# Halving the first loads of a two-layer decoder kernel, moving its bias rows to another queue, and storing the last result by batch

## The chip, the cores and the metric

The kernel runs on one core of a Trainium2 chip. Times are device microseconds (us) from the start to the end of one execution; the time of a kernel is the median of its timed runs. A separate execution was taken by the hardware profiler, and every row and duration below comes from that one.

## The reference

Two decoder layers on 8 sequences of 256 tokens by 256 features, in float32. Each layer is self-attention, cross-attention to a context of 120 tokens, and a feed-forward block, each followed by a layer norm of the sum. The change touches the first block alone, and the store of the last one:

```python
def _L0_attn_ref(x, kernel, WO):
    q = jnp.einsum('bsm,hmd->bhsd', x, kernel[0])
    k = jnp.einsum('bsm,hmd->bhsd', x, kernel[1])
    v = jnp.einsum('bsm,hmd->bhsd', x, kernel[2])
    ...
    scores = jnp.einsum('bhsd,bhtd->bhst', q, k) * scale
    attn = jax.nn.softmax(scores, axis=-1)
    out = jnp.einsum('bhst,bhtd->bhsd', attn, v)
...
x = _layernorm(x + _L0_attn_ref(x, L0_attn_kernel, L0_attn_WO), axis=-1)
...
x = _layernorm(x + _L1_ffn_ref(x, ...), axis=-1)
```

There are 16 heads of 64, so each of the three slices of `L0_attn_kernel` is a 256 by 1024 matrix of 1 MB.

## The kernel before

The 8 sequences go through in four passes of two (`NB = 2`, `NI = 4`); a pass holds 512 tokens, that is `T = 4` tiles of 128 tokens, `TS = 2` per sequence. Features stand in `KD = 2` slices of 128. Every engine has its own instruction stream, written out by hand in the order in which it runs; the streams meet at semaphores (`wait_ge`, `then_inc`). Nothing is reordered by a planner.

Before the first pass, the SP queue issues the loads in the order in which it is written (lines 460 to 475): the turned input of the two sequences (`turned_x`, features on the partitions), 256 KB each; then value, query and key weights `wv0`, `wq0`, `wk0`, each in two slices of 512 KB, whose runs in memory are one head's 64 floats; then the context, the input `xa`, the output weights and those of the later blocks of layer 0. A DMA counts 16 on its semaphore. Beside it the ScalarE queue issues five loads (lines 1527 to 1531): three small ones of bias columns, then `rows`, twelve bias and gain rows of 256 floats copied to all 128 partitions (1536 KB), then `scalars`. VectorE waits for `rows` and `scalars` together (`got["rows"]`, line 2089) before it makes six small constants, and after that waits for the first scores.

TensorE starts with `project_first` (line 593). It waits for all of `wv0` and for both halves of `turned_x`, and then makes the values: eight groups of 128 tokens by 512 features, over `n = 0..7` with token tile `t = n // 2` and half of the features `h = n % 2`. A group is two products of 128x128 by 128x512 over the two slices of features; each stands in the trace as two instructions, since the numbers are float32 (32 for the eight groups). Groups go alternately to two PSUM banks, and from the third on each waits until ScalarE has copied the group two before it (`v0_kept`, from `keep_first`, line 1244). Then come eight groups of queries and eight of keys over the full 512 tokens, then the scores, and from there one pass after another. `load_turned_x` of the next pass waits for the last key group of this one.

The last pass ends batch by batch on VectorE (line 2107 on): the norm of sequence 0 is applied, then the sums, the statistics and the norm of sequence 1; each `apply_norm` counts up `normed["out"]`. SP waits for both and stores 512 KB at once (`store`, line 454), and waits for that store.

Of the kernel before, what the change touches and what calls it, by code (L numbers as in the profile page):

```python
# [11 lines left out]
P = 128  # L12
# [32 lines left out]
def decoder(nc, I, out):  # L45
    x = I["x"]
    B, S, D = x.shape
# [3 lines left out]
    KD = D // P  # L51
# [18 lines left out]
    with ExitStack() as es:  # L70
# [3 lines left out]
        def signal(name, per=1):  # L74
            return Signal(es.enter_context(nc.semaphore(name)), per)
# [225 lines left out]

        x_in, xt_in = signal("x_in", 16), signal("xt_in", 16 * NB)
        ctx_in_s = signal("ctx_in", 16 * NB)
        got = {n: signal("got_" + n) for n in ("v0", "qk0", "o0", "x0", "ffn0", "ctx", "attn1", "x1", "ffn1",
                                               "cols", "rows")}
# [149 lines left out]

        @blk.sync
        def _(sp):
            load_turned_x(sp, 0)  # L460
            for n, w in ((2, wv0), (0, wq0), (1, wk0)):
                for k in range(KD):
                    sp.dma_start(w[:, k, :].rearrange("p (h d) -> p h d", h=H),
                                 I["L0_attn_kernel"][n, :, k * P:(k + 1) * P, :].rearrange("h p d -> p h d")
                                 ).then_inc(got["v0" if n == 2 else "qk0"].sem, 16)
            load_ctx(sp, 0)
            load_x(sp, 0)
            wo = I["L0_attn_WO"][0].rearrange("(d j e) m -> e d j m", j=J, e=2)
            for e in range(2):
                sp.dma_start(wo0[e * DH0:(e + 1) * DH0, :, :], wo[e]).then_inc(got["o0"].sem, 16)  # L470
            for n in xw_names:
                sp.dma_start(x0w[n][:, :, :], by_tile(I["L0_xattn_" + n], KD)).then_inc(got["x0"].sem, 16)
            for n, k in (("gate", KD), ("up", KD), ("down", C0)):
                sp.dma_start(wn[n][:, :, :], by_tile(I["L0_ffn_w_" + n], k)).then_inc(got["ffn0"].sem, 16)
            load_turned_x(sp, 1)
            sp.wait_ge(w_rounded.sem, 3)
            for n in ("Wk1", "Wk2", "Wv1", "Wv2"):
                sp.dma_start(c_w[n][:, :, :], by_tile(I["L1_xattn_" + n], KD)).then_inc(got["ctx"].sem, 16)
            for n in ("Wv", "Wo"):
                sp.dma_start(m_w[n][:, :, :], by_tile(I["L1_attn_" + n], KD)).then_inc(got["attn1"].sem, 16)  # L480
            sp.dma_start(w1[:, :, :], by_tile(I["L1_attn_W1"], KD)).then_inc(got["attn1"].sem, 16)
            sp.dma_start(w2[:, :, :], by_tile(I["L1_attn_W2"], C1)).then_inc(got["attn1"].sem, 16)
            for e, n in enumerate(("Wf", "Wi")):
                for k in range(KD):
                    sp.dma_start(wfi[:, k, e:e + 1], I["L1_attn_" + n][k * P:(k + 1) * P, :]).then_inc(got["attn1"].sem, 16)
            for n in ("Wq", "Wo"):
                sp.dma_start(c_w[n][:, :, :], by_tile(I["L1_xattn_" + n], KD)).then_inc(got["x1"].sem, 16)
            for t, n, k in ((n_w1, "cn_w1", KD), (n_w2, "cn_w2", KD), (g_w1, "gc_w1", KD)):
                sp.dma_start(t[:, :, :], by_tile(I["L1_ffn_" + n], k)).then_inc(got["ffn1"].sem, 16)
            for t, n in ((n_w3, "cn_w3"), (n_w4, "cn_w4"), (g_w2, "gc_w2"), (g_w3, "gc_w3")):  # L490
                sp.dma_start(t[:, :], I["L1_ffn_" + n]).then_inc(got["ffn1"].sem, 16)

            load_x(sp, 1)
            load_ctx(sp, 1)

            for it in range(1, NI - 1):
                load_turned_x(sp, it + 1)
                store(sp, it - 1)
                load_x(sp, it + 1)
                load_ctx(sp, it + 1)  # L500
            store(sp, NI - 2)
            store(sp, NI - 1)
            sp.wait_ge(out_sent.sem, 16 * NI)


        @blk.tensor
        def _(pe):
# [84 lines left out]

            def project_first():

                pe.wait_ge(got["v0"].sem, 16 * KD)
                for n in range(2 * T):
                    if n == 0:
                        pe.wait_ge(xt_in.sem, 16 * NB)
                    elif n > 1:
                        pe.wait_ge(v0_kept.sem, n - 1)  # L600
                    t, h = n // 2, n % 2
                    for k in range(KD):
                        mm = pe.matmul(bank(7 - n % 2), turned_x[:, k, t * P:(t + 1) * P],
                                       wv0[:, k, h * 512:(h + 1) * 512], start=(k == 0), stop=(k == KD - 1))
                    mm.then_inc(v0_done.sem, 1)
                pe.wait_ge(got["qk0"].sem, 16 * 2 * KD)
                for j in range(J):
                    if j < 2:
                        pe.wait_ge(v0_kept.sem, 2 * T - 1 + j)
                    else:  # L610
                        pe.wait_ge(q0_kept.sem, j - 1)
                    for k in range(KD):
                        mm = pe.matmul(bank(7 - j % 2), wq0[:, k, j * P:(j + 1) * P], turned_x[:, k, :],
                                       start=(k == 0), stop=(k == KD - 1))
                    mm.then_inc(q0_done.sem, 1)
                for j in range(J):
                    if j < 2:
                        pe.wait_ge(q0_kept.sem, J - 1 + j)
                    else:
                        pe.wait_ge(k0_kept.sem, j - 1)  # L620
                    for k in range(KD):
                        mm = pe.matmul(bank(7 - j % 2), wk0[:, k, j * P:(j + 1) * P], turned_x[:, k, :],
                                       start=(k == 0), stop=(k == KD - 1))
                    mm.then_inc(k0_done.sem, 1)
# [586 lines left out]
        def _(act):  # L1211
# [32 lines left out]
            def keep_first():  # L1244
                for n in range(2 * T):
                    act.wait_ge(v0_done.sem, n + 1)
                    act.copy(v0[:, n // 2, n % 2 * 512:(n % 2 + 1) * 512], bank(7 - n % 2)).then_inc(v0_kept.sem, 1)
                for j in range(J):
                    act.wait_ge(q0_done.sem, j + 1)
                    act.mul(q0[:, j, :], bank(7 - j % 2), W0).then_inc(q0_kept.sem, 1)  # L1250
                for j in range(J):
                    act.wait_ge(k0_done.sem, j + 1)
                    act.copy(k0[:, j, :, :].rearrange("p b s -> p (b s)"), bank(7 - j % 2)).then_inc(k0_kept.sem, 1)
# [273 lines left out]
            act.dma_start(cols[:, :], I["cols"]).then_inc(got["cols"].sem, 16)  # L1527
            act.dma_start(n_b3[:, :], I["L1_ffn_cn_b3"].rearrange("(p c) -> p c", c=1)).then_inc(got["cols"].sem, 16)
            act.dma_start(g_b2[:, :], I["L1_ffn_gc_b2"].rearrange("(p c) -> p c", c=1)).then_inc(got["cols"].sem, 16)
            act.dma_start(rows[:, :, :], I["rows"].partition_broadcast(P)).then_inc(got["rows"].sem, 16)  # L1530
            act.dma_start(scalars[:, :], I["scalars"].partition_broadcast(P)).then_inc(got["rows"].sem, 16)
            def one_pass(it, last=None, then=None):
                attn0(it, last)
# [785 lines left out]
```

## Time and profile before

| | us |
|---|---|
| timed runs: median (lowest to highest) of 3 | 1265.72 (1265.17 to 1266.19) |
| the profiled execution: its own time | 1278.1 |
| its span | 1275.9 |
| TensorE busy in it | 1075.6 (84%) |
| VectorE busy | 765.4 (60%) |
| ScalarE busy | 649.0 (51%) |
| GpSimd busy | 331.1 (26%) |
| TensorE's mean granted clock, share of full | 0.922 |

The profiled execution took 2.2 us outside its span and is 12.4 us longer than the median of the timed runs. Differences of before and after are looked for in its span; a duration of it need not be that of a timed run to the last tenth. In the rows below PE is TensorE, PEld its weight loads, DVE VectorE, ACT ScalarE, POOL GpSimd, and SPq and ACTq the queues that issue DMAs. "Idle before" names what ended an engine's wait. PEclk is the granted clock as a share of the full 2.4 GHz. Matmuls overlap, so the start-to-start distance, not the duration, is what one costs.

### The profile page before, as it was taken

What the parts mean: (1) busy time and instruction counts of PE and PEld (TensorE: products, weight loads), DVE (VectorE), ACT (ScalarE), POOL (GpSimd) and SP (SyncE); (2) the same over time, 40 slices, a digit from 0 to 9 for tenths busy, and PEclk for the clock granted to TensorE, in tenths of its full rate; (3) what the DMA queues carried; (4) which work ended last, traced back from release to release, by engine and by line L of the source; (5) the groups of instructions that cost most, each with busy time, mean ns of one, the idle gap of its engine ahead of it and who ended that gap; (6) DMA issues with size and microseconds to landing.
All of it is one profiled execution on the core that took longest, in us unless ns stands there. A gap on an engine that the chain in (4) does not pass through costs nothing.

```text
span 1275.9 us, 19390 instructions
## 1 busy us (share of the span) xinstructions
PE 1075.6 (84%) x7058; PEld 692.6 (54%) x7058; DVE 765.4 (60%) x1834; ACT 649.0 (51%) x1744; POOL 331.1 (26%) x670
## 2 busy tenths in 40 slices
PE   5987988899879998899788998899778987788874
PEld 2454645674545654585454655585454664475452
DVE  0177476556647558565847657664856747864655
ACT  1465345247347744546647734554637724544622
POOL 1056301231115520222025530221124630131012
PEclk9988999897689999999989999998899998998676
DMA  9302200000000000000000000000000000000000
GB/s 238 132 2 90 62 1 9 1 0 2 1 1 18 18 17 1 8 1 1 1 1 18 18 17 2 8 1 1 1 1 1 18 1 2 1 1 1 1 1 17
DMA packets 30446, 22.76 MB, mean 18 GB/s; under 512 B 16656, under 2 KB 29456, under 8 KB 30224
## 3 DMA queue, kind: packets, MB, share of 16 engines
q1 hardware_dynamic: 29760, 19.93, 5.7%
q10 hardware_dynamic: 592, 1.59, 0.3%
q8 instruction: 57, 0.93, 0.3%
q14 instruction: 37, 0.30, 0.1%
HBM read 19.42 MB, written 2.10 MB: 17 GB/s over the span
## 4 chain that ended last, share of the span: by engine, by line
PE 59%; DVE 18%; ACT 11%; issue 5%; POOL 4%; DMA 1%; SPq 0%; POOLq 0%; DVEq 0%; ACTq 0%
PE PS L542 8%; PE PS L529 4%; PE PS L690 4%; PE PS L929 4%; ACT work L1445 4%; PE PS L589 3%; POOL work L2149 3%; PE PS L778 3%; PE PS L572 3%; PE PS L659 2%; PE PS L942 2%; PE PS L676 2%; PE PS L903 2%; PE PS L977 2%; PE PS L641 2%
## 5 line engine op out<-in xcount | busy, mean ns | idle before, releaser
L2123 POOL TENSOR_TENSOR rstd<-var,minus_half 128x2 f32<-128x2 f32 x64 | 45.8, 715 | 464.1 <-DVE var L1569 464.1
L1445 ACT ACTIVATE work<-PS,nmax 120x256 f32<-120x256 f32 x256 | 117.7, 489 | 44.8 <-DVE nmax L1984 44.5
L2149 POOL TENSOR_SCALAR work<-work,inv 128x256 f32<-128x256 f32 x256 | 125.3, 507 | 0.0
L1984 DVE TENSOR_REDUCE nmax<-PS 120x2 f32<-120x512 f32 x128 | 82.0, 685 | 71.0 <-PE PS L929 70.8
L1628 DVE TENSOR_REDUCE nmax<-PS 128x2 f32<-128x512 f32 x128 | 82.2, 684 | 67.3 <-PE PS L641 67.2
L1261 ACT ACTIVATE work<-PS,nmax 128x256 f32<-128x256 f32 x256 | 118.1, 482 | 4.1 <-DVE nmax L1628 4.0
L2118 POOL TENSOR_TENSOR pool_pause<-minus_half 128x1 f32<-128x1 f32 x96 | 30.1, 314 | 263.1 <-DVE inv L1635 138.7
L929 PE MATMUL PS<-x_room 32*120 32x256 f32 x512 | 72.7, 462 | 14.9 <-ACT work L1445 11.2
L676 PE MATMUL PS<-work 128*64 128x256 f32 x512 | 71.2, 400 | 9.6 <-DVE work L1639 9.5
L641 PE MATMUL PS<-work 64*128 64x256 f32 x512 | 72.7, 400 | 1.9 <-ACT work L1261 1.9
L929 PEld LDWEIGHTS PS<-x_room 32*120 32x120 f32 x512 | 44.5, 207 | 41.9 <-issue 33.1
L690 PE MATMUL PS<-wo,work 128*128 128x256 f32 x256 | 60.9, 392 | 2.7 <-ACT work L1271 2.7
L659 PEld LDWEIGHTS PS<-ident,work 64*128 64x128 f32 x1024 | 38.4, 144 | 41.3 <-POOL work L2149 35.2
L1639 DVE COPY work<-PS 128x512 f32<-128x512 f32 x64 | 43.9, 685 | 27.6 <-PE PS L659 27.2
L659 PE MATMUL PS<-ident,work 64*128 64x64 f32 x1024 | 47.4, 235 | 13.8 <-POOL work L2149 12.9
L1267 ACT COPY work<-PS 128x512 f32<-128x512 f32 x64 | 37.6, 588 | 40.7 <-PE PS L659 40.0
L977 PE MATMUL PS<-work,late 128*128 128x256 f32 x96 | 33.9, 486 | 29.0 <-ACT work L1473 29.0
L1735 DVE TENSOR_REDUCE maxx<-PS 128x8 f32<-128x960 f32 x32 | 36.9, 1153 | 34.7 <-PE PS L749 34.6
L942 PE MATMUL PS<-work,v1p 120*32 120x256 f32 x512 | 42.2, 455 | 18.2 <-ACT work L1445 9.6
L1217 ACT COPY turned_a<-PS 128x512 f32<-128x512 f32 x24 | 14.2, 591 | 84.0 <-PE PS L512 84.0
L1445 ACT ACTIVATION_READ_ACCUMULATOR work<-PS,nmax 120x1 f32 x256 | 56.6, 221 | 0.0
L1261 ACT ACTIVATION_READ_ACCUMULATOR work<-PS,nmax 128x1 f32 x256 | 54.7, 214 | 0.0
(278 smaller groups left out, 2441.3 us busy)
## 6 DMA issues: line engine op xcount, KB each, us to landing
turned_x<-in_xT_dram SPq DMA_DIRECT2D x8, 256.0 KB, 3.1
xa<-in_x_dram SPq DMA_DIRECT2D x4, 512.0 KB, 4.5
out_dram<-x_room SPq DMA_DIRECT2D x4, 512.0 KB, 3.0
rows<-in_rows_dram ACTq DMA_DIRECT2D x1, 1536.0 KB, 8.3
late<-in_L_attn_W_dram SPq DMA_DIRECT2D x2, 768.0 KB, 8.0
wv<-in_L_attn_kernel_dram SPq DMA_DIRECT2D x2, 512.0 KB, 11.3
wq<-in_L_attn_kernel_dram SPq DMA_DIRECT2D x2, 512.0 KB, 7.8
wk<-in_L_attn_kernel_dram SPq DMA_DIRECT2D x2, 512.0 KB, 7.5
```

Source lines behind the costliest of these rows:

```text
L542: mm = pe.matmul(bank(n)[:, (t % 2) * width:(t % 2 + 1) * width], lhs[:, k, t * P:(t + 1) * P], weight[:, k, :], start=(k == 0), stop=(k = ...
L641: mm = pe.matmul(bank(2 * (u % 2) + hh)[:, st * S:(st + 1) * S], q0[rows, j, b * S + st * P:b * S + (st + 1) * P], k0[rows, j, b, :], star ...
L659: mm = pe.transpose(bank(4 + g)[:, place:place + 64], e0[rows, u % 2, st, hh, tt * P:(tt + 1) * P], ident[rows, rows])
L676: mm = pe.matmul(bank(6)[hh * DH0:(hh + 1) * DH0, b * S:(b + 1) * S], v0[:, TS * b + tt, (2 * j + hh) * DH0:(2 * j + hh + 1) * DH0], e0t[: ...
L690: mm = pe.matmul(bank(t // 2)[:, (t % 2) * D:(t % 2 + 1) * D], o0t[:, j, t * P:(t + 1) * P], wo0[:, j, :], start=(j == 0), stop=(j == J - 1))
L929: mm = pe.matmul(bank(SCORE_1[r])[0:M, kv * S:(kv + 1) * S], k1m[g % 2][rows, kv, par, :], q1[rows, c, b * S:(b + 1) * S], start=True, sto ...
L942: mm = pe.matmul(bank(2)[32 * r:32 * r + 32, g % 2 * S:(g % 2 + 1) * S], v1p[:, par, r, kv, :, :], e1[:, par, r, kv, :], start=(par == 0 a ...
L1261: op = act.activation(e0[:, u % 2, st, hh, :], bank(2 * (u % 2) + hh)[:, st * S:(st + 1) * S], ACT.Exp, bias=nmax0[:, u % 2, hh, st:st + 1 ...
L1445: op = act.activation(e1[:, par, r, kv, :], bank(SCORE_1[r])[0:M, kv * S:(kv + 1) * S], ACT.Exp, bias=nmax1[:, par, r, kv:kv + 1], accum_o ...
L1628: dve.tensor_reduce(nmax0[:, u % 2, hh, :], bank(2 * (u % 2) + hh).rearrange("p (t s) -> p t s", t=TS), AX.X, ALU.max, negate=True).then_i ...
L1984: dve.tensor_reduce(nmax1[:, par, r, :], bank(SCORE_1[r])[0:M, :].rearrange("p (v s) -> p v s", v=2), AX.X, ALU.max, negate=True).then_inc ...
L2149: op = pool.tensor_scalar(e0[:, u % 2, st, hh, :], e0[:, u % 2, st, hh, :], inv0[:, u % 2, hh, st:st + 1], 1.0, ALU.mult, ALU.mult)
```

## The change

SP now issues the first half of `turned_x` (sequence 0) and the value weights of heads 0 to 7 in two DMAs of 256 KB, all three counting on a new semaphore `opening`; behind them sequence 1 and the value weights of heads 8 to 15; then the query and key weights as before, and then `rows`, which leaves the ScalarE queue. TensorE makes the four token tiles for the first half of the features, then the four for the second; it waits for `opening` at group 0, for sequence 1 at group 2 and for the other half of the weights at group 4. ScalarE copies the groups to where they now belong. The last result is stored sequence by sequence.

```diff
@@ -301,7 +301,7 @@
 
 
 
-        x_in, xt_in = signal("x_in", 16), signal("xt_in", 16 * NB)
+        x_in, xt_in, opening = signal("x_in", 16), Signal(es.enter_context(nc.semaphore("xt_in")), 16 * NB, -16), signal("opening")
         ctx_in_s = signal("ctx_in", 16 * NB)
         got = {n: signal("got_" + n) for n in ("v0", "qk0", "o0", "x0", "ffn0", "ctx", "attn1", "x1", "ffn1",
                                                "cols", "rows")}
@@ -457,12 +457,20 @@
 
         @blk.sync
         def _(sp):
-            load_turned_x(sp, 0)
-            for n, w in ((2, wv0), (0, wq0), (1, wk0)):
+            for half in range(2):
+                sp.dma_start(turned_x[:, :, half * S:(half + 1) * S], I["xT"][half].rearrange("(k p) s -> p k s", p=P)
+                             ).then_inc((xt_in if half else opening).sem, 16)
+                for k in range(KD):
+                    heads = slice(half * H // 2, (half + 1) * H // 2)
+                    sp.dma_start(wv0[:, k, half * 512:(half + 1) * 512].rearrange("p (h d) -> p h d", h=H // 2),
+                                 I["L0_attn_kernel"][2, heads, k * P:(k + 1) * P, :].rearrange("h p d -> p h d")
+                                 ).then_inc((got["v0"] if half else opening).sem, 16)
+            for n, w in ((0, wq0), (1, wk0)):
                 for k in range(KD):
                     sp.dma_start(w[:, k, :].rearrange("p (h d) -> p h d", h=H),
                                  I["L0_attn_kernel"][n, :, k * P:(k + 1) * P, :].rearrange("h p d -> p h d")
-                                 ).then_inc(got["v0" if n == 2 else "qk0"].sem, 16)
+                                 ).then_inc(got["qk0"].sem, 16)
+            sp.dma_start(rows[:, :, :], I["rows"].partition_broadcast(P)).then_inc(got["rows"].sem, 16)
             load_ctx(sp, 0)
             load_x(sp, 0)
             wo = I["L0_attn_WO"][0].rearrange("(d j e) m -> e d j m", j=J, e=2)
@@ -499,8 +507,11 @@
                 load_x(sp, it + 1)
                 load_ctx(sp, it + 1)
             store(sp, NI - 2)
-            store(sp, NI - 1)
-            sp.wait_ge(out_sent.sem, 16 * NI)
+            for b in range(NB):
+                sp.wait_ge(normed["out"].sem, normed["out"].at(NI - 1, b + 1))
+                sp.dma_start(out[(NI - 1) * NB + b].rearrange("(t p) d -> p t d", p=P), y[:, TS * b:TS * b + TS, :]
+                             ).then_inc(out_sent.sem, 16)
+            sp.wait_ge(out_sent.sem, 16 * (NI + 1))
 
 
         @blk.tensor
@@ -592,13 +603,16 @@
 
             def project_first():
 
-                pe.wait_ge(got["v0"].sem, 16 * KD)
                 for n in range(2 * T):
+                    h, t = n // T, n % T
                     if n == 0:
-                        pe.wait_ge(xt_in.sem, 16 * NB)
-                    elif n > 1:
+                        pe.wait_ge(opening.sem, 16 * (1 + KD))
+                    if n == TS:
+                        pe.wait_ge(xt_in.sem, 16)
+                    if n == T:
+                        pe.wait_ge(got["v0"].sem, 16 * KD)
+                    if n > 1:
                         pe.wait_ge(v0_kept.sem, n - 1)
-                    t, h = n // 2, n % 2
                     for k in range(KD):
                         mm = pe.matmul(bank(7 - n % 2), turned_x[:, k, t * P:(t + 1) * P],
                                        wv0[:, k, h * 512:(h + 1) * 512], start=(k == 0), stop=(k == KD - 1))
@@ -1244,7 +1258,7 @@
             def keep_first():
                 for n in range(2 * T):
                     act.wait_ge(v0_done.sem, n + 1)
-                    act.copy(v0[:, n // 2, n % 2 * 512:(n % 2 + 1) * 512], bank(7 - n % 2)).then_inc(v0_kept.sem, 1)
+                    act.copy(v0[:, n % T, n // T * 512:(n // T + 1) * 512], bank(7 - n % 2)).then_inc(v0_kept.sem, 1)
                 for j in range(J):
                     act.wait_ge(q0_done.sem, j + 1)
                     act.mul(q0[:, j, :], bank(7 - j % 2), W0).then_inc(q0_kept.sem, 1)
@@ -1527,7 +1541,6 @@
             act.dma_start(cols[:, :], I["cols"]).then_inc(got["cols"].sem, 16)
             act.dma_start(n_b3[:, :], I["L1_ffn_cn_b3"].rearrange("(p c) -> p c", c=1)).then_inc(got["cols"].sem, 16)
             act.dma_start(g_b2[:, :], I["L1_ffn_gc_b2"].rearrange("(p c) -> p c", c=1)).then_inc(got["cols"].sem, 16)
-            act.dma_start(rows[:, :, :], I["rows"].partition_broadcast(P)).then_inc(got["rows"].sem, 16)
             act.dma_start(scalars[:, :], I["scalars"].partition_broadcast(P)).then_inc(got["rows"].sem, 16)
             def one_pass(it, last=None, then=None):
                 attn0(it, last)
```

How SP's queue stands at the start of the program, before:

```order
L443 DMA turned_x<-in_xT_dram 128x2x256 x2
L463 DMA wv0<-in_L0_attn_kernel_dram 128x16x64 x2
L463 DMA wq0<-in_L0_attn_kernel_dram 128x16x64 x2
L463 DMA wk0<-in_L0_attn_kernel_dram 128x16x64 x2
L451 DMA ctxt<-in_ctxT_dram 128x2x120 x2
L436 DMA xa<-in_x_dram 128x4x256
L470 DMA wo0<-in_L0_attn_WO_dram 64x8x256 x2
```

and now:

```order
L461 DMA turned_x<-in_xT_dram 128x2x256
L465 DMA wv0<-in_L0_attn_kernel_dram 128x8x64 x2
L461 DMA turned_x<-in_xT_dram 128x2x256
L465 DMA wv0<-in_L0_attn_kernel_dram 128x8x64 x2
L470 DMA wq0<-in_L0_attn_kernel_dram 128x16x64 x2
L470 DMA wk0<-in_L0_attn_kernel_dram 128x16x64 x2
L473 DMA rows<-in_rows_dram 128x3072
L451 DMA ctxt<-in_ctxT_dram 128x2x120 x2
```

The two loads of `wv0` became four of half the size with half of `turned_x` between them, and `rows` stands between the key weights and the context.

TensorE's first groups with what they wait for, before:

```order
L603 MATMUL PS<-wv0,turned_x 128x512 [waits xt_in,got_v0]
L603 MATMUL PS<-wv0,turned_x 128x512 x3
L603 MATMUL PS<-wv0,turned_x 128x512 [waits v0_kept]
L603 MATMUL PS<-wv0,turned_x 128x512
L603 MATMUL PS<-wv0,turned_x 128x512 [waits v0_kept]
```

and now:

```order
L617 MATMUL PS<-wv0,turned_x 128x512 [waits opening]
L617 MATMUL PS<-wv0,turned_x 128x512 x3
L617 MATMUL PS<-wv0,turned_x 128x512 [waits v0_kept,xt_in]
L617 MATMUL PS<-wv0,turned_x 128x512
L617 MATMUL PS<-wv0,turned_x 128x512 [waits v0_kept]
L617 MATMUL PS<-wv0,turned_x 128x512
L617 MATMUL PS<-wv0,turned_x 128x512 [waits v0_kept,got_v0]
```

Number, size and place of the products are the same; the first waits for half of the loads, and two later ones wait for the rest.

## Rows read from the trace of the kernel before

**Rows 1.** Chain of work that ended last, 0 to 70 us: start, length, what

```profile
1.78 0.46 SPq L463
...
2.29 11.98 DMA wv<-in_L_attn_kernel_dram
...
14.31 16.46 PE PS L603 x32
30.77 13.73 PE PS L613 x32
44.50 13.73 PE PS L622 x32
58.24 1.11 PE PS L641 x8
```

**Rows 2.** DMA issues of short stretches from 0.7 us: sizes, us from issue to landing

```profile
turned_x<-in_xT_dram SPq DMA_DIRECT2D x1, 256.0 KB, 3.0
...
wv<-in_L_attn_kernel_dram SPq DMA_DIRECT2D x1, 512.0 KB, 10.6
...
wv<-in_L_attn_kernel_dram SPq DMA_DIRECT2D x1, 512.0 KB, 12.0
...
rows<-in_rows_dram ACTq DMA_DIRECT2D x1, 1536.0 KB, 8.3
...
wk<-in_L_attn_kernel_dram SPq DMA_DIRECT2D x1, 512.0 KB, 7.5
...
late<-in_L_ffn_w_down_dram SPq DMA_DIRECT2D x1, 1024.0 KB, 14.2
```

**Rows 3.** Issues in order of time: start, length of issue, queue and line

```profile
0.79 0.94 SPq L443 DMA_DIRECT2D turned_x<-in_xT_dram  x2
1.78 6.18 SPq L463 DMA_DIRECT2D wv<-in_L_attn_kernel_dram  x2
...
2.48 0.60 ACTq L1530 DMA_DIRECT2D rows<-in_rows_dram  x1
...
13.98 4.69 SPq L463 DMA_DIRECT2D wk<-in_L_attn_kernel_dram  x2
...
28.54 1.21 SPq L474 DMA_DIRECT2D late<-in_L_ffn_w_down_dram  x1
```

**Rows 4.** Stretches of 2 us: busy by engine, PEclk, DMA share, GB/s last

```profile
4.00:6.00 2.00, 0.00 (x0) 0.00 (x0) 0.00 (x0) 0.00 (x0) 0.97 (x6) 1.00 0.82 189
6.00:8.00 2.00, 0.00 (x0) 0.00 (x0) 0.00 (x0) 0.00 (x0) 0.00 (x0) 1.00 1.05 396
8.00:10.00 2.00, 0.00 (x0) 0.00 (x0) 0.00 (x0) 0.00 (x0) 0.00 (x0) 1.00 0.98 404
...
42.00:44.00 2.00, 2.00 (x6) 0.85 (x5) 0.00 (x0) 0.60 (x1) 0.00 (x0) 1.00 0.01 3
```

**Rows 5.** TensorE's weight loads and ScalarE's copies at the start, in order of time

```profile
17.89 0.33 PEld L603 LDWEIGHTS PS<-wv,turned_x 128*128 128x128 f32 x1 [0.52 <-issue]
...
18.74 0.33 PEld L603 LDWEIGHTS PS<-wv,turned_x 128*128 128x128 f32 x1 [0.52 <-issue]
19.45 0.19 PEld L603 LDWEIGHTS PS<-wv,turned_x 128*128 128x128 f32 x1 [0.38 <-issue]
19.47 0.59 ACT L1247 COPY work<-PS 128x512 f32<-128x512 f32 x1
20.11 0.39 PEld L603 LDWEIGHTS PS<-wv,turned_x 128*128 128x128 f32 x2 [0.47 <-ACT work L1247]
...
25.66 0.58 ACT L1247 COPY work<-PS 128x512 f32<-128x512 f32 x1 [1.13 <-PE PS L603]
...
27.37 0.58 ACT L1247 COPY work<-PS 128x512 f32<-128x512 f32 x1 [1.13 <-PE PS L603]
```

**Rows 6.** VectorE's first work, and its first read of the feed-forward weights

```profile
59.33 2.48 DVE L1628 TENSOR_REDUCE nmax<-PS 128x2 f32<-128x512 f32 x4 [46.94 <-PE PS L641]
...
70.94 2.28 DVE L1602 TENSOR_REDUCE w_sum<-late 128x1 f32<-128x2048 f32 x1
```

**Rows 7.** The end of the program in order of time: norms and the last store

```profile
1266.89 0.74 DVE L1575 TENSOR_SCALAR x_room<-res,mv,rstd 128x256 f32<-128x256 f32 x2 [0.40 <-POOL rstd L2123]
...
1271.82 0.74 DVE L1575 TENSOR_SCALAR x_room<-res,mv,rstd 128x256 f32<-128x256 f32 x2 [0.81 <-POOL rstd L2123]
1272.59 0.38 SPq L456 DMA_DIRECT2D out_dram<-x_room  x1
```

**Rows 8.** DMA view of 1270 to 1276 us: rates in 40 slices, and the store

```profile
GB/s 0 0 0 0 0 0 0 0 0 0 0 0 0 0 0 0 0 0 0 0 0 0 0 157 348 355 335 355 355 335 362 341 335 212 7 0 0 0 0 0
...
out_dram<-x_room SPq DMA_DIRECT2D x1, 512.0 KB, 2.9
```

## The prediction

> **What bounds the kernel now.** I read the chain of waits first. Its head is [rows 1]: from 2.29 to 14.27 us the program waits for the second load of the value weights, and from 14.31 us TensorE works without a gap through values (16.46 us), queries (13.73) and keys (13.73) until the scores begin at 58.24. So the start of the program is bound by one landing, and then by TensorE. Next the DMA view: which transfers stand ahead of that landing and how fast they go [rows 2 to 4]. Then TensorE and ScalarE at the start, to see when the third and the fifth group are due, since these get new waits [rows 5]. Then who else reads what was loaded [rows 6], and last the end of the program [rows 7, 8]. Everything between the scores of the first pass and the last norm is left as it was, so the question is how much earlier the first matmul can start, whether this arrives at the end, and what the last store gives.
>
> **The change part by part.**
>
> Why the weights land at 14.3 now. SP issues the two inputs from 0.79 us, and the weights at 1.78 and 2.29 [rows 1, 3]. They land at 1.78 + 10.6 = 12.4 and 2.29 + 12.0 = 14.3 [rows 2]. The bytes alone don't explain it: inputs and value weights are 1.5 MB. In 4 to 6 us the DMAs moved 189 GB/s, in 6 to 10 us 396 and 404 [rows 4]; the jump is the 1536 KB of bias rows, issued at 2.48 and landed at 2.48 + 8.3 = 10.8 [rows 2, 3]. The weights come in runs of 256 bytes, the bias rows in runs of 12 KB, and while these pass, the weights hardly move.
>
> Start of TensorE, after. It needs one input half and two quarters of the weights, 256 + 512 KB, and nothing large beside them. The first input was issued at 0.79 and landed 3.0 us later, at 3.8 [rows 2, 3]; it stays first. The 512 KB of weights (524,288 bytes) follow it in the queue, at the 189 GB/s of 4 to 6 us, the stretch with weights in it before the bias rows [rows 4]: 2.8 us, so 6.6 us. The bounds: at the 404 GB/s of 8 to 10 us they take 1.3 us, hence 5.1. On the late side I take the landing that the whole first slice of 512 KB had, 12.4, and subtract only what the bias rows take at about 400 GB/s, 1,572,864 bytes / 400 = 3.9: 8.5 us. Its bytes are as many as the two quarters now. I take 6.6, since the 189 GB/s is for just these runs at just this place; the second key slice, at the end of a long line of such runs, supports it: two of them take 4.69 us to issue, with the queue full [rows 3], 2.35 us for 512 KB. The gain is 14.3 - 6.6 = **7.7 us** (5.8 to 9.2).
>
> The new waits inside the values cost nothing. Before, the third group started at 20.11, 5.8 us after the first, when ScalarE's first copy ended [rows 5]; later groups are 1.71 apart (copies at 25.66 and 27.37 [rows 5]). So group 2 is due at 6.6 + 5.8 = 12.4 and group 4 at 6.6 + 5.8 + 2 x 1.71 = 15.8. Behind the opening there are 256 KB of input and 512 KB of weights, which at the same 189 GB/s take 1.4 and 2.8 us: they are in at 8.0 and 10.8. The cover is 4.4 and 5.0 us; if it were gone, what is late would be lost one for one. What is queued behind these waits is TensorE's whole stream, and ScalarE's copies wait for it.
>
> Order of groups. 32 instructions before, 32 after, with the same operands' shapes; two banks in turn, the same copies on ScalarE of 0.58 us against 1.71 us per group. Nothing.
>
> Query and key weights. The key weights are issued by 18.7 [rows 3], and the last lands some 7.5 us [rows 2] after the middle of that, at about 24; nothing new stands ahead of them, and the bias rows no longer share the engines. Queries are due at 6.6 + 16.5 = 23.1, keys at 36.8, and the query weights went ahead of the key weights by 1 MB, that is by 4.7 us: at 19. The cover shrinks from 11 to 4 us, and stays.
>
> Bias rows. On ScalarE's queue an issue of 0.60 us goes [rows 3], before anything ScalarE has to do. On SP's, it stands ahead of context, input, output weights and the rest. All those loads together end when they did, since the bytes are the same: by 42 us the DMA share is 0.01 [rows 4], the last, w_down, lands at 28.54 + 14.2 = 42.7 [rows 2, 3]. VectorE now waits for the bias rows until about 28 instead of 12; its next work is due at 59.33 - 7.7 = 51.6 [rows 6]. The feed-forward weights are first read at 70.94 - 7.7 = 63.2 [rows 6]. So the cover is 20 us and the cost is nothing.
>
> From there on every event waits, directly or over others, for TensorE's first groups, so all moves by 7.7 us.
>
> Clock. At the start weight loads are 0.85 us apart until 18.74, and from 19.45 on their duration is 0.19 instead of 0.33 [rows 5]: TensorE runs at 1.2 GHz for some 5.1 us after its first matmul and then at 2.4 (the PEclk of that stretch doesn't show it). It idles before it now as it did then, so I keep the values phase at 16.46 us, 2.73 more than the queries. If the slow stretch is absent or twice as long, the start is 2.7 better or worse; a third of that is what I allow. The Trainium skill, TensorE: Matmul & The Clock Gate (part 1, the HAM clock gate), says that the number of slow matmuls at a kernel's start differs from run to run of one kernel. One trace can't show that; the timed runs, 1.0 us apart, leave little room for it, and the sum would be the same.
>
> Last store. It was issued at 1272.59 and landed 2.9 us later; its bytes moved from about 1273.4 to 1275.1 at 335 to 362 GB/s [rows 7, 8]. Now the first sequence is ready at 1266.89 + 0.74 = 1267.6, five us earlier, and only 256 KB are left at 1272.59. At 350 GB/s they take 0.75 instead of 1.5 us; issue and the time after the last byte stay. Gain **0.7 us**; at worst nothing, at best half of the 2.9, 1.4. The Trainium skill, DMA: Bandwidth & Descriptors (anatomy of one DMA), has a fixed part of about 2.0 us and the bytes at 436 GB/s. By it a store of 524,288 bytes takes 3.2 us (the trace: 2.9) and the halving is worth an estimated 0.6. The same formula for the opening's 786,432 bytes from 0.79 us would give 4.6 us and a sum 2.0 us lower than mine; there the rows contradict, since runs of 256 bytes went at 189 GB/s.
>
> **Sum.** 7.7 + 0.7 = 8.4 us off the profiled span of 1275.9: 1267.5. That execution is 12.4 us longer than the median, but neither term is one that its clock could have stretched: both are DMA times. So 1265.72 - 8.4 = **1257.3 us**.
>
> **The rivals.**
>
> Fast opening: with the bias rows gone the small runs go at what the queue reached in 8 to 10 us, the first matmul is at 5.1. Gain 9.2 + 0.7: 1255.8. Against it, the 189 GB/s stretch held next to none of the bias rows. 8%.
>
> Slow opening: the first slice's landing carried a delay of its own, not the bias rows' alone, and the opening is at 8.5 or later. Gain 5.8 + 0.7: 1259.2. For it: between 4 and 6 us the engines were only 0.82 busy, so the transfers were held by something. 10%.
>
> Nothing arrives: the bias rows delay something behind them on SP that the first pass waits for. It would have to be 20 us late for the feed-forward weights. Then the first pass gets back what it gained, and 1265.0 remains. 4%.
>
> Slower: the clock. If the earlier and broken-up start keeps TensorE at 1.2 GHz through the values, each of the 32 instructions costs 0.85 instead of 0.43 us: 27.2 instead of 16.46, 10.7 more, against 8.4 gained: 1268.0. It decides where some 20 of them more than before are slow. Against it: the cover of 4.4 and 5.0 us leaves no new gap, so TensorE does just what it did after its start before. 3%.
>
> **How the numbers follow.** The forecast, an opening between 5.5 and 8 us and a shift that arrives whole, has 75%: 1256 to 1259. The two other openings have 18%, the rest 7%. For the range I go from the fast opening with 1.4 us for the store and 0.9 for the clock, 1265.7 - 9.2 - 1.4 - 0.9 = 1254.2, to the slow one with nothing for the store and 0.9 for the clock, 1265.7 - 5.8 + 0.9 = 1260.8. 0.2% is 2.5 us, about what a measurement of this kernel can tell from no change. All three openings are faster by more than this: 0.93. Within it are the case in which nothing arrives and very late openings: 0.04. Slower: 0.03.
>
> **What the profile after would show.** The first matmul near 6.6 us, waiting for `wv` or `turned_x`; no idle time of TensorE by a DMA at the third and fifth group; the values again 16.5 us, scores at 50.5; VectorE's wait for `rows` ending near 28 and followed by a wait for TensorE; DMA share near zero again from 42; a store of 256 KB at about 1267.6 less the shift, and one that lands near 2.2 us after its issue. I would be wrong if the 256-byte runs at the head of the queue go slower alone than beside others, if sequence 1's input or the other half of the weights ended a wait of TensorE, or if the later passes in the new profile took longer than in the old.

## The result

The changed kernel took 1258.42 us (median of 20 runs), the kernel before 1266.66 (20 runs of its own). The ratio is 0.9942, with a 95% interval from 0.9915 to 0.9968: 7.3 us faster, between 4.1 and 10.8. The prediction was 8.4 us off, to 1257.3, in a range from 1254.2 to 1260.8.

| | before | after |
|---|---|---|
| profiled execution: time | 1278.1 | 1251.83 |
| its span | 1275.9 | 1249.7 |
| TensorE's mean granted clock | 0.922 | 0.940 |
| first matmul | 14.31 | 6.92 |
| values take | 16.46 | 16.43 |
| first scores | 58.24 | 50.82 |
| last store, issue to landing | 2.9 | 2.1 |

The two spans differ by 26.2 us, three times what the timed runs give. The difference that the change made is seen at both ends. First the chain of waits of after, its first 52 us (start, length, what); these lines answer to [rows 1]:

```profile
1.78 5.09 DMA wv<-in_L_attn_kernel_dram
...
6.92 3.79 PE PS L617 x4
...
10.79 1.28 ACT L1261
...
12.08 0.59 ACT work L1261
...
12.81 10.54 PE PS L617 x24
23.35 13.73 PE PS L627 x32
37.08 13.73 PE PS L636 x32
50.82 1.11 PE PS L655 x8
```

The wait for the value weights ends at 6.88 instead of 14.27 us. Queries and keys take 13.73 us each as before, so the scores come 7.42 us earlier. The small pieces between 10.7 and 12.8 are ScalarE's table load and first copy, on which the third group waits; in [rows 5] they stood at the same distance from the start.

The rates of the DMAs of after, in stretches of 2 us (columns as in [rows 4], GB/s last):

```profile
4.00:6.00 2.00, 0.00 (x0) 0.00 (x0) 0.00 (x0) 0.00 (x0) 0.99 (x6) 1.00 1.05 194
6.00:8.00 2.00, 1.08 (x2) 0.56 (x3) 0.00 (x0) 0.00 (x0) 0.00 (x0) 1.00 1.21 282
8.00:10.00 2.00, 2.00 (x4) 0.95 (x3) 0.00 (x0) 0.00 (x0) 0.00 (x0) 1.00 1.36 218
...
18.00:20.00 2.00, 2.00 (x6) 0.95 (x5) 0.00 (x0) 0.63 (x2) 0.00 (x0) 1.00 1.13 351
20.00:22.00 2.00, 2.00 (x6) 0.86 (x5) 0.00 (x0) 0.87 (x2) 0.00 (x0) 1.00 1.02 381
```

194 GB/s while the opening is loaded, then 218 for long stretches of 256-byte runs; the 400 GB/s of 6 to 10 us are gone, and the bias rows pass from 18 to 22 us instead. VectorE waited for them until 23.7 us, and this held nothing up: its first work after that wait, and its first work on scores, 28 us later, as [rows 6] before:

```profile
23.73 0.15 DVE L2104 TENSOR_SCALAR half_b<-scalars 128x1 f32<-128x1 f32 x1 [21.48 <-DMA rows<-in_rows_dram]
...
51.91 2.48 DVE L1641 TENSOR_REDUCE nmax<-PS 128x2 f32<-128x512 f32 x4 [27.70 <-PE PS L655]
```

Last, the end of after: the DMA view of 1244 to 1250 us, in 40 slices as in [rows 8], with the norm ahead of the store:

```profile
1246.38 0.73 DVE L1588 TENSOR_SCALAR x_room<-res,mv,rstd 128x256 f32<-128x256 f32 x2 [0.81 <-POOL rstd L2136]
...
GB/s 0 0 0 0 0 0 0 0 0 0 0 0 0 0 0 0 0 0 0 0 0 0 0 0 0 0 41 287 348 348 369 301 55 0 0 0 0 0 0 0
...
out_dram<-x_room SPq DMA_DIRECT2D x1, 256.0 KB, 2.1
```

The bytes of the last store move for some 0.8 us instead of 1.6, at the same rate, and it lands 2.1 us after its issue.

**Where the other 18 us of the spans went.** Each timed execution comes with its mean granted clock. Over 179 executions of eleven kernels (the two of this study and the nine variants below; for the 20 runs of before beside the result no clock is on record, so its 71 here come from the later sessions) I fitted one span per kernel and one slope for all: a mean clock lower by 0.01 goes with a span longer by 10.0 us (plus or minus 0.3), and what remains is 0.9 us per execution. Slow executions (over 1.5% above the fastest of their kernel; 16 of 195) are left out of the ratios and of this fit; with them the slope is the same and no gain below moves by more than 0.4 us. In one kernel's 20 executions the clock went from 0.922 to 0.941 and the span from 1268.2 to 1249.2. So 0.018 of clock between the two profiled executions is 18 us, and 26.2 - 18 = 8.2 us are the change's; 7.4 + 0.8 at the two ends. In this way, "at equal clock" below, the kernel after is 8.1 us faster (7.7 to 8.5) over 31 executions against 71 of before: 7.9 +- 0.5 from the 19 beside the result, 8.3 +- 0.5 from the 12 of the repetition. The slope is a relation among executions, not an experiment on the clock.

### The profile page after: what moved, and what is told of

Same layout as the page of the kernel before. It is cut to its first block, busy times and chain, and to the rows that moved or that the text cites. A ratio compares the mean times of both kernels' runs of the same rounds, so it can differ in the third digit from the quotient of the medians.

```text
span 1249.7 us, 19394 instructions
## 1 busy us (share of the span) xinstructions
PE 1056.4 (85%) x7058; PEld 683.4 (55%) x7058; DVE 764.8 (61%) x1834; ACT 649.8 (52%) x1744; POOL 331.5 (27%) x670
## 4 chain that ended last, share of the span: by engine, by line
PE 58%; DVE 19%; ACT 12%; issue 6%; POOL 4%; DMA 0%; SPq 0%; POOLq 0%; DVEq 0%; ACTq 0%
PE PS L553 8%; PE PS L540 4%; PE PS L704 4%; ACT work L1459 4%; PE PS L943 4%; POOL work L2162 3%; PE PS L600 3%; PE PS L583 3%; PE PS L792 3%; PE PS L673 2%; PE PS L917 2%; PE PS L690 2%; PE PS L956 2%; PE PS L991 2%; PE PS L655 2%
## 5 line engine op out<-in xcount | busy, mean ns | idle before, releaser
L943 PE MATMUL PS<-x_room 32*120 32x256 f32 x512 | 68.3, 437 | 16.3 <-ACT work L1459 12.5
L1231 ACT COPY turned_a<-PS 128x512 f32<-128x512 f32 x24 | 14.2, 592 | 84.0 <-PE PS L523 83.9
L1588 DVE TENSOR_SCALAR x_room<-res,mv,rstd 128x256 f32<-128x256 f32 x96 | 36.3, 420 | 30.6 <-POOL rstd L2136 30.6
```

The costliest lines, as they stand in the source:

```text
L943: mm = pe.matmul(bank(SCORE_1[r])[0:M, kv * S:(kv + 1) * S], k1m[g % 2][rows, kv, par, :], q1[rows, c, b * S:(b + 1) * S], start=True, sto ...
```

## The experiments

All gains are against the kernel before. "At equal clock" is the fitted value with its 95% interval.

| kernel | first matmul | scores | ratio of timed runs | gain at equal clock |
|---|---|---|---|---|
| before | 14.31 | 58.24 | | |
| bias rows moved alone | 10.30 | 54.13 | 0.9967 (0.9929 to 1.0006) | 4.3 +- 0.6 |
| halves alone | 11.78 | 56.18 | 0.9951 (0.9902 to 1.0000) | 3.1 +- 0.7 |
| store by batch alone | 14.61 | 58.44 | 0.9995 (0.9946 to 1.0045) | 0.9 +- 0.7 |
| after | 6.92 | 50.82 | 0.9942 (0.9915 to 0.9968) | 8.1 +- 0.4 |
| after, again | 7.26 | 51.64 | 0.9941 (0.9920 to 0.9962) | (in the line above) |
| other half of the weights last | 8.08 | 56.31 | 0.9985 (0.9940 to 1.0031) | 4.5 +- 0.6 |
| bias rows late on ScalarE's queue | 6.95 | 51.69 | 0.9934 (0.9902 to 0.9966) | 6.9 +- 0.6 |
| with extra products | 7.87 | 49.97 | 0.9888 (0.9830 to 0.9945) | 9.7 +- 0.7 |
| wait by slice | 5.26 | 49.71 | 0.9945 (0.9910 to 0.9981) | 10.2 +- 0.6 |
| slice and three extra products | 5.06 | 49.60 | 0.9894 (0.9833 to 0.9956) | 10.2 +- 0.8 |
| slice, five products, early table | 5.47 | 47.53 | 0.9929 (0.9892 to 0.9965) | 10.8 +- 0.6 |

**The bias rows alone.**

```diff
-            act.dma_start(rows[:, :, :], I["rows"].partition_broadcast(P)).then_inc(got["rows"].sem, 16)
...
+            sp.dma_start(rows[:, :, :], I["rows"].partition_broadcast(P)).then_inc(got["rows"].sem, 16)
             load_ctx(sp, 0)
```

> The kernel before with one edit: the bias rows go from the ScalarE queue to SP's, behind the key weights. Theory (the bias rows held the weights up by the 4 us in which they passed): the inputs land at 3.8 and 4.5 us, and 1 MB of weights behind them at about 200 GB/s lands near 10.0; the first matmul starts there instead of at 14.3, scores start near 54, about 4.3 us off. Rival (the weights were late by their own length, and halving is what helped): the first matmul stays near 14.

The chain of waits of this kernel:

```profile
2.28 7.97 DMA wv<-in_L_attn_kernel_dram
...
10.30 3.79 PE PS L604 x4
...
54.13 1.11 PE PS L642 x8
```

The first matmul came at 10.30, 4.0 us earlier, with all of the loads still waited for at once. The bias rows did hold the weights up by about the time in which they passed, and the first expectation held.

**Halves alone.** The changed kernel with these two edits, the bias rows' issue back on ScalarE's queue and one store:

```diff
-            sp.dma_start(rows[:, :, :], I["rows"].partition_broadcast(P)).then_inc(got["rows"].sem, 16)
+            act.dma_start(rows[:, :, :], I["rows"].partition_broadcast(P)).then_inc(got["rows"].sem, 16)
...
+            store(sp, NI - 1)
+            sp.wait_ge(out_sent.sem, 16 * NI)
```

> The changed kernel with the bias rows back on the ScalarE queue and the last result stored at once, so only the halving of inputs and value weights is left. Theory (the opening's 768 KB are through before the bias rows' packets start near 6.3 us): first matmul at 7 to 7.5 us, the other half of the value weights lands near 14.3 and no wait appears at the fifth group, due at 16; scores start near 51, 7 us off. Rival (both parts are needed, the bias rows overlap the opening): first matmul at 9 to 10 us.

Both expectations missed: the first matmul came at 11.78, later than either. The chain, and the rates of the first 16 us in slices of 0.4 us:

```profile
1.78 9.95 DMA wv<-in_L_attn_kernel_dram
...
11.78 16.94 PE PS L613 x32
...
GB/s 1 0 0 0 28 69 252 336 270 269 237 207 161 124 213 240 344 468 438 437 445 321 348 369 310 230 185 293 330 301 224 175 184 209 265 266 259 225 216 215
```

The first slice of the weights landed 3.7 us after its issue, before the bias rows came; the second, issued half a microsecond later, landed 9.95 us after its issue. The rise from 240 to 468 GB/s begins at 6.4 us, and I read it as the bias rows' packets, which began while the last of the second slice was still under way: it came in at 11.73, 1.1 us after the bias rows (2.47 + 8.1 = 10.6). In after it was in at 6.87, so by this reading it missed by about half a microsecond here, and that cost 4.9 us. The rates don't tell whose packets they are; that the time of the bias rows does it is tested by the run with the same queue and a later issue, below. The three parts add up within the noise: 4.3, 3.1 and 0.9 us at equal clock make 8.3, against 8.1 for all of them. At the first matmul they give 4.0 and 2.5, together 6.5, against 7.4 and 7.05 in the two profiles of after.

**The store alone.** The loop over `b` of the diff in the kernel before, nothing else.

> The kernel before with the last result stored sequence by sequence and nothing else changed. Theory: first matmul at 14.3 as before, the last DMA carries 256 KB and lands 2.1 us after its issue instead of 2.9: 0.8 us off, too little for the timed runs. Rival (the fixed part rules, no gain): it lands after 2.9 us.

The last DMA carried 256 KB and landed 2.1 us after its issue, as in after. 0.9 +- 0.7 us at equal clock agrees with 0.8; the timed ratio alone could not have told it.

**What the cover at the fifth group is worth.** The loads of the weights' other half stand behind query and key weights:

```diff
             for half in range(2):
                 ...
-                for k in range(KD):
+                if half == 0:
+                    load_values(0)
...
                                  ).then_inc(got["qk0"].sem, 16)
+            load_values(1)
```

> The changed kernel with the other half of the value weights loaded behind query and key weights, to see what the cover of the fifth group is worth. Theory: the first matmul stays at 6.9; 2 MB at 218 GB/s stand ahead of that half, it lands near 19.7, while the fifth group is due near 16.1: TensorE waits 3.6 us for a DMA there, and scores start near 54.4 instead of 50.8. Rival (the landing's cover is larger than worked out, or the order in the queue doesn't set the order of landing): no wait, scores at 50.8.

TensorE in order of time, then two weight loads behind the wait and the first at full clock:

```profile
8.08 9.85 PE L621 MATMUL PS<-wv,turned_x 128*128 128x512 f32 x16 [8.08 <-DMA wv<-in_L_attn_kernel_dram]
20.02 8.83 PE L621 MATMUL PS<-wv,turned_x 128*128 128x512 f32 x16 [2.09 <-DMA wv<-in_L_attn_kernel_dram]
...
22.40 0.34 PEld L621 LDWEIGHTS PS<-wv,turned_x 128*128 128x128 f32 x1 [0.52 <-issue]
23.26 0.34 PEld L621 LDWEIGHTS PS<-wv,turned_x 128*128 128x128 f32 x1 [0.52 <-issue]
23.97 0.19 PEld L621 LDWEIGHTS PS<-wv,turned_x 128*128 128x128 f32 x1 [0.37 <-issue]
```

Ahead of the wait the loads were 0.19 us long and 0.43 apart from 13.94 on, so the clock had been up. The half landed at 19.97, as worked out (19.7). The wait was 2.1 us and not 3.6, since this execution's opening landed at 8.0 and not 6.9. But the scores came at 56.31, 1.9 us later than the expected 54.4: after the wait TensorE ran at 1.2 GHz again until 23.97 (weight loads of 0.34 us, 0.86 apart), and the last 16 instructions took 8.83 us instead of 6.9. A wait of 2 us at this place costs 4; at equal clock this kernel stands 3.6 us behind after.

**The bias rows on ScalarE's queue, but later.**

```diff
-            sp.dma_start(rows[:, :, :], I["rows"].partition_broadcast(P)).then_inc(got["rows"].sem, 16)
...
+            act.wait_ge(opening.sem, 16 * (1 + KD))
+            act.dma_start(rows[:, :, :], I["rows"].partition_broadcast(P)).then_inc(got["rows"].sem, 16)
             act.wait_ge(got["cols"].sem, 16 * N_COLS)
```

> The changed kernel with the bias rows on the ScalarE queue again, but issued only once the opening has landed: the same queue as before, another time. Theory (what counts is when the bias rows' packets are under way, not whose queue issues them): first matmul between 6.9 and 8.1 us as in the changed kernel, and the second half of the value weights lands near 14, before it is due at 16; scores start near 51 to 52. Rival (rows on a second queue hold the small runs up whenever they are there, long enough for the fifth group): TensorE waits for a DMA at the fifth group, scores at 54 or later.

```profile
6.95 16.72 PE L616 MATMUL PS<-wv,turned_x 128*128 128x512 f32 x32 [6.95 <-DMA wv<-in_L_attn_kernel_dram]
23.95 6.28 PE L626 MATMUL PS<-turned_x,wq 128*128 128x512 f32 x14 [0.29 <-DMA wk<-in_L_attn_kernel_dram]
```

The first matmul came at 6.95: on the same queue as before, issued at 6.92 instead of 2.48, the bias rows do not hold the opening up, so moving them in time is enough. Whether the queue matters for bias rows issued at the same time was not tested. There was no wait at the fifth group. A wait came where neither side expected one: 0.29 us at the first query group, for the key weights, whose last slice landed at 16.3 + 7.6 = 23.9. At equal clock the kernel gains 6.9 us, 1.2 less than after, so the place behind the key weights is the better one. Where the 1.2 us arise isn't shown: the wait is 0.3, and the scores come 0.9 us after those of the first profile of after, but level with those of the second (51.64).

**What the low clock at the start costs.** The changed kernel with

```diff
             def project_first():
 
+                pe.wait_ge(zeroed.sem, 1)
+                for i in range(5):
+                    pe.matmul(bank(5)[:, 0:256], warm[:, 0:P], warm[:, P:P + 256], start=True, stop=True)
```

where `warm` is a new tile that VectorE fills first.

> The changed kernel with five extra products of 128x128 by 128x256 of a tile of ones, made by TensorE while it waits for the opening; their result is never read. It measures what the low clock at the start costs. They last from about 2 to 6.3 us. Theory (the clock rises by what TensorE did before): the first real group runs at 2.4 GHz or gets there soon, the values take about 14 us instead of 16.4, scores start near 48.4 and the kernel is 2.4 us faster than the changed one. Rival (the clock rises only some time after the real work starts): the values take 16.4 us again, no gain.

```profile
1.37 4.63 PE L609 MATMUL PS<-warm 128*128 128x256 f32 x10 [1.37 <-DVE warm L2101]
7.87 3.70 PE L621 MATMUL PS<-wv,turned_x 128*128 128x512 f32 x8 [1.87 <-DMA wv<-in_L_attn_kernel_dram]
11.97 10.54 PE L621 MATMUL PS<-wv,turned_x 128*128 128x512 f32 x24 [0.39 <-ACT work L1265]
```

The first group of four took 2.0 us here and 3.8 in after, and the values 14.6 us instead of 16.4, although TensorE had been idle for 1.87 us just ahead. So the clock's rise follows TensorE's earlier work and not the start of the real one, and 1.8 us of the 2.7 that I had put down to it can be had. Most of the rest is the table load, which holds the third group: its loads stand at 10.55 and, three on, at 12.47, which is 1.92 us for three steps that take 1.29 at full clock, so 0.6 us of the remaining 0.9. The scores came at 49.97 and not at the expected 48.4, since this opening landed 0.95 us later than in the first profile of after, and since the table load was still in the way.

**Waiting by slice.** The first group waits for one slice of the weights, its second half for the other:

```diff
-                                 ).then_inc((got["v0"] if half else opening).sem, 16)
+                                 ).then_inc((got["v0"] if half else (opening2 if k else opening)).sem, 16)
...
-                        pe.wait_ge(opening.sem, 16 * (1 + KD))
+                        pe.wait_ge(opening.sem, 16 * 2)
...
                     for k in range(KD):
+                        if n == 0 and k == 1:
+                            pe.wait_ge(opening2.sem, 16)
```

> The changed kernel, but the first group waits for the first slice of the weights (and the input), and only its second half for the second slice, on a semaphore of its own. Theory (in the changed kernel the slices landed at 5.2 and 6.9 us): first matmul at 5.2, the second slice is due at 5.2 + 1.7 = 6.9, when it lands; scores start near 49.1 instead of 50.8, 1.7 us off. Rival (the clock's rise is not tied to the start, or the second slice lands later because the first one waits no longer): gain below 0.8 us.

The first matmul came at 5.26 and the scores at 49.71, 1.1 us before the first profile of after and 1.9 before the second; at equal clock it gains 10.2, 2.1 more than after. The scores stayed 0.6 us short of the expected 49.1, but the gain is more than the rival's 0.8.

> Both: the wait by slice, and three instead of five extra products ahead of it, from about 2 to 4.6 us. Theory: first real matmul at 5.2, the second slice at 6.9 becomes what is waited for, the rest at 2.4 GHz: scores near 47.5, 3.3 us before the changed kernel's. Rival (the gains don't add, since the wait for the second slice takes back one): scores near 48.4, as with the extra products alone.

Scores at 49.60. The extra products ended at 4.3, the first real product began at 5.06 and the second slice landed at 7.36. The values still took longer than at full clock (30 instructions in 14.72 us, 12.9 at 0.43): the weight loads were 0.85 us apart again until 10.13. This kernel differs from the last one in fewer products and in the two pauses behind them, of 0.8 and 0.3 us; it doesn't tell which of these did it. The scores came 1.2 us later than even the second expectation (48.4), and practically when they come with the wait by slice alone (49.71).

**All together,** with one small ScalarE copy ahead of the real ones:

```diff
+            act.wait_ge(zeroed.sem, 1)
+            act.copy(table_probe[:, 0:1], warm[:, 0:1])
             act.wait_ge(got["cols"].sem, 16 * N_COLS)
             keep_first()
```

> The changed kernel with the wait by slice, the five extra products, and one small copy on ScalarE ahead of the first real one, so that its table is loaded while it waits (1.28 us of load stood between the first group and its copy). Theory: the clock is up, the first real matmul at 6.1 to 6.9, the second slice is waited for until 6.9 to 7.8, the values take 13.8 us from there less half a group, scores start at 47.5 to 48.5, some 3 us before the changed kernel's. Rival (the table load was hidden, and slice and clock don't add): scores at 49.6, as with fewer extra products.

```profile
1.37 4.27 PE L610 MATMUL PS<-warm 128*128 128x256 f32 x10 [1.37 <-DVE warm L2106]
5.47 1.02 PE L624 MATMUL PS<-wv,turned_x 128*128 128x512 f32 x2
6.92 13.14 PE L624 MATMUL PS<-wv,turned_x 128*128 128x512 f32 x30 [0.43 <-DMA wv<-in_L_attn_kernel_dram]
...
19.74 0.35 PEld L634 LDWEIGHTS PS<-turned_x,wq 128*128 128x128 f32 x2 [0.51 <-DMA wk<-in_L_attn_kernel_dram]
```

From 6.92 on all loads are 0.19 us long and 0.43 apart, the table was loaded at 3.1 us, and the scores come at 47.53, 3.3 us before those of the first profile of after: the first expectation held. At equal clock it gains 10.8 us against 8.1, but it isn't told apart from the wait by slice (10.2 +- 0.6). The timed ratios, 0.9929 against 0.9941 of the changed kernel on the same chip, don't tell those two apart either, and the median of all its runs there, 1263.51, is above the 1262.20 of the changed kernel. That it beats the changed kernel in plain time is therefore not shown. The last line shows the next limit: the first query weights now wait for the key weights. It costs nothing yet, since the next load, at 20.33, stands where it would without the wait, but the cover of the key weights is used up.

**After, again.**

> The changed kernel once more, unchanged, beside the two others on the same chip. Theory: the opening lands between 6.9 and 8.1 us (the spread seen in three kernels with the same first loads), scores start at 50.8 to 52, and at equal granted clock its span is 7.4 + 0.8 = about 8 us below that of before. Rival (part of the measured gain is the clock's, by chance): at equal clock it is 4 us or less.

First matmul at 7.26, scores at 51.64, ratio 0.9941, and 8.3 +- 0.5 us at equal clock: the gain repeats in another session, and the first expectation held. The opening's last landing over the five kernels that load alike up to there and wait for both slices at once (the two of after, the late bias rows, other half last, extra products) was followed by a first matmul at 6.92, 7.26, 6.95, 8.08 and 7.87. One trace gives such a landing to about 0.6 us either way.

## Why the prediction was right

**Start of TensorE.** Predicted 6.6 with ends at 5.1 and 8.5; measured 6.92 and 7.26, and 6.95 to 8.08 in the variants. The chosen rate was right, 189 GB/s against 194. The mechanism that I gave, the bias rows hold 256-byte runs up, was confirmed by moving them alone, and the late end's subtraction (3.9 us for the bias rows) by the same run: 14.3 - 10.3 = 4.0. The gain was a little too high, 7.7 against 7.4, since the landing was 0.3 us later. All five landings that can be compared came after the 6.6 that I took, on average at 7.4, so the estimate was at their early edge.

**New waits inside the values.** No wait at groups 2 and 4, as predicted. That the wait would be lost "one for one" if the cover were gone was wrong: with the half loaded last, a wait of 2.1 us cost another 1.9 through the clock.

**Query and key weights.** This step was wrong in its working, and by luck of two errors not in its result. I compared the query weights' landing with the due time of the queries. But the first query group waits for query and key weights together (`got["qk0"]`, line 606 before). I had the last key slice at about 24 and the queries due at 23.1; read rightly, that was a wait of 0.9 us. It didn't come, because the key weights moved too: their issues are held back by the queue ahead (one takes 2.3 to 2.5 us, where the first slice of the value weights took 0.46 [rows 1]), and with the bias rows gone their last slice was issued at 12.0 instead of 16.3 and landed at 19.6, 3.7 us before it was due. With the bias rows on ScalarE's queue behind the opening it landed at 23.9, and the wait appeared.

**Bias rows.** Landed at 14.55 + 9.1 = 23.7 instead of the 28 that I had, and w_down, the last load, at 28.93 + 14.2 = 43.1, 0.4 us later than before. The cover for VectorE was 28 us where I had 20.

**Clock at the start.** Kept at 16.46, measured 16.43, and 16.9 in the repetition. That the first two agree is partly luck, since the 2.7 us over the queries' 13.73 have other parts in each profile. In after the loads at 1.2 GHz ended after 4.2 us (5.1 before), and then the third group waited for ScalarE's first copy:

```profile
11.58 0.19 PEld L617 LDWEIGHTS PS<-wv,turned_x 128*128 128x128 f32 x1 [0.24 <-issue]
12.78 0.30 PEld L617 LDWEIGHTS PS<-wv,turned_x 128*128 128x128 f32 x2 [1.01 <-issue]
13.32 0.19 PEld L617 LDWEIGHTS PS<-wv,turned_x 128*128 128x128 f32 x1 [0.24 <-issue]
```

From 11.58 to 13.32 are three steps, which take 1.29 us at 0.43: 0.45 us went there, and some 2.0 to the clock; the last 0.3 stand in the run at full clock too (13.14 us for 30 instructions). In the repetition the slow loads lasted 6.0 us, there was no such wait, and the clock took 2.9. So this stretch does differ between executions of one kernel, and by no more than the 0.9 us that I had allowed. It is the part of the start that a change can still take.

**Store.** 0.7 predicted, 0.8 in the trace. The Trainium skill's DMA: Bandwidth & Descriptors (anatomy of one DMA), with its fixed 2.0 us, gives an estimated 2.6 for 256 KB; the trace has 2.1, so its fixed part is too large here, while its estimated 0.6 for the difference is near the 0.8 of the traces. The page has this fit for DMAs that GpSimd issues, which I hadn't said; these stores are issued by SP.

**The sum.** 8.4 predicted; 8.2 by the trace, 8.1 +- 0.4 at equal clock, 7.3 (4.1 to 10.8) by the timed ratio. The median fell on 1258.4 within the range of 1254.2 to 1260.8. The kernel before came out at 1266.66 over 20 runs where I had started from 1265.72 over three, and these 0.9 us are most of the 1.1 by which 1257.3 was too low. What failed is the side remark on the profiled span: I expected 1267.5 and it was 1249.7. I had carried the 12.4 us between the profiled execution and the median over as if they belonged to profiling. By the fitted relation they are what a mean clock lower by 0.012 goes with, and another execution has another clock.

**The rivals.** Fast and slow opening didn't come; the latest opening with these loads, 8.08, stays ahead of the 8.5 of the slow one. Nothing arrives and the clock's loss didn't come either, though the run with the half loaded last shows what the latter would look like.

## What to carry to other kernels

At a program's start, look at what else the DMA engines carry while the first matmul's operands are under way: a large transfer with long runs, issued on another queue a microsecond later, held loads with 256-byte runs up by about all of its own length (4.0 us, against 3.9 for its bytes at 400 GB/s). Issue such a transfer later; in the one run that kept its queue, this alone was enough. And let the first product wait only for its own slices. Where executions differ by more than the change is worth, compare them at their granted clock, and trust the two ends of the trace before the span.

## What the hardware showed that I had not expected

- Nearly all of the spread between executions of one program goes with the mean granted clock: 10.0 us of span per 0.01 of it, with 0.9 us left over, in a range of 0.916 to 0.941.
- TensorE's clock was up at 7.87 us after extra products from 1.37 to 6.0 us and an idle time of 1.87; but after an idle time of 2.1 us in the middle of the values it was at 1.2 GHz again for 4 us. The Trainium skill, TensorE: Matmul & The Clock Gate (part 1, the HAM clock gate), has the number of slow matmuls vary from run to run of one kernel with when the work falls; the slow stretch of 4.2 us in one profile of after and 6.0 in the other agrees with that. For what follows a pause, two traces can't say more.
- The second slice of the opening landed 5.1 to 6.3 us after its issue in eight executions with the same loads ahead of it (5.1 in four of them), and 10.0 with the bias rows issued 0.7 us behind it.
